# Routed tiles numbered by the token block of their first row, and the results of eight of sixteen token tiles gathered and added within the expert loop

## The reference, cut to what matters

```python
x = x + 0.5 * _L0_ffn_ref(_layernorm(x, axis=-1), ...)
x = x + _L0_attn_ref(_layernorm(x, axis=-1), ...)
x = x + 0.5 * _L0_ffn_ref(_layernorm(x, axis=-1), ...)
```

```python
scores = jax.nn.sigmoid(jnp.einsum('ed,btd->bte', gate_w, x)) + gate_b
weights, indices = jax.lax.top_k(scores, 4)
weights = weights / weights.sum(-1, keepdims=True)
shared_out = jax.nn.silu(x @ w1_shared) * (x @ w3_shared) @ w2_shared
h3 = jax.nn.silu(jnp.einsum('btd,edc->btec', x, w1_routed) * jnp.einsum('btd,edc->btec', x, w3_routed))
experts_out = jnp.einsum('btec,ecd->bted', h3, w2_routed)
return shared_out + jnp.einsum('bted,bte->btd', experts_out, router_probs)
```

## Time and profile before

| what | us |
|---|---|
| median of three runs | 695.49 |
| fastest and slowest run | 694.51, 701.63 |
| the profiled execution, span of the trace | 702.1 |
| VectorE, ScalarE, GpSimd, TensorE busy in it | 443.5, 372.6, 350.9, 509.0 |

### The profile page before, as it was taken

One profiled execution on the slowest core, in us unless ns is written; L12 is line 12 of the kernel. 1 busy time (PEld: TensorE's weight loads), 2 busy tenths in 40 slices (PEclk: granted clock), 3 DMA queues, 4 the chain that ended last, 5 costly groups with the idle time before them and its releaser, 6 DMA issues.

```text
span 702.1 us, 14339 instructions
## 1 busy us (share of the span) xinstructions
PE 509.0 (73%) x3204; PEld 462.6 (66%) x3205; DVE 443.5 (63%) x1453; ACT 372.6 (53%) x1132; POOL 350.9 (50%) x362
## 2 busy tenths in 40 slices
PE   4867699999999802538286924999999999632702
PEld 4845599999999801426264912999999999521501
DVE  5887477777777523448397587677777777221516
ACT  3777377777777701426175645677777777200000
POOL 2997544444444077464402233544444442475764
PEclk9987799999999955568599965899999999755555
DMA  9951254444445344232201440344444444433633
GB/s 304 392 201 51 83 152 134 134 131 128 131 133 129 102 130 126 82 113 74 77 0 35 144 167 15 99 134 135 128 130 132 134 125 113 132 115 92 177 98 105
DMA packets 61135, 88.11 MB, mean 126 GB/s; under 512 B 9499, under 2 KB 46363, under 8 KB 61107
## 3 DMA queue, kind: packets, MB, share of 16 engines
q0 software_dynamic: 13728, 37.50, 21.2%
q1 hardware_dynamic: 47379, 50.29, 20.8%
HBM read 57.22 MB, written 30.54 MB: 125 GB/s over the span
## 4 chain that ended last, share of the span: by engine, by line
PE 56%; DVE 13%; issue 9%; ACT 6%; DVEq 5%; another core or an unknown queue 4%; DMA 3%; POOL 3%; SPq 0%; ACTq 0%
PE bank L1164 26%; PE bank L1215 13%; PE bank L1186 5%; DVE xres L972 3%; PE bank L1379 3%; PE bank L1226 3%; PE bank L1225 3%; POOL mamba_room L488 2%; DVEq L972 2%; DVEq L971 1%; DVE lg L802 1%; DMA ys_scratch<-ring_f 1%; PE bank L1237 1%; DVE ring_f L948 1%
## 5 line engine op out<-in xcount | busy, mean ns | idle before, releaser
L478 POOL DMA_INDIRECT ring_f<-xn_scratch,tokidx x158 | 152.8, 967 | 170.3 <-PE bank L1186 150.0
L1164 PE MATMUL bank<-w_routed,ring_r 128*128 x948 | 194.6, 341 | 0.0
L488 POOL DMA_INDIRECT mamba_room<-ys_scratch,si x128 | 124.2, 971 | 97.3 <-issue 36.3
L1164 PEld LDWEIGHTS bank<-w_routed,ring_r 128*128 128x128 f32 x948 | 152.4, 192 | 1.0 <-issue 0.8
L1215 PE MATMUL bank<-w_routed,ring_r 128*128 x790 | 119.7, 282 | 0.7 <-DVE ring_r L832 0.6
L1215 PEld LDWEIGHTS bank<-w_routed,ring_r 128*128 128x128 f32 x790 | 110.1, 188 | 1.6 <-issue 1.6
L565 ACT ACTIVATE ring_r<-bank 128x256 fp32r<-128x256 f32 x158 | 60.8, 385 | 73.9 <-PE bank L1226 73.9
L972 DVE SCALAR_TENSOR_TENSOR xres<-mamba_room,wk,xres 128x256 f32<-128x256 f32 (+1 forms) x128 | 57.4, 481 | 52.5 <-issue 43.1
L830 DVE TENSOR_TENSOR ring_r<-bank,ring_r 128x128 fp32r<-128x128 f32 x158 | 46.1, 292 | 63.7 <-ACT ring_r L565 63.6
L822 DVE TENSOR_TENSOR ring_r<-bank,ring_r 128x256 fp32r<-128x256 f32 x158 | 67.1, 425 | 14.2 <-ACT ring_r L556 8.1
L1379 PE MATMUL bank<-mamba_room,stage 128*128 128x256 f32 (+1 forms) x144 | 42.5, 451 | 43.8 <-ACT mamba_room L754 30.0
(11 more groups left out here) (147 smaller groups left out, 755.6 us busy)
## 6 DMA issues: line engine op xcount, KB each, us to landing
ys_scratch<-ring_f SPq DMA_DIRECT2D x158, 128.0 KB
raw_routed<-in_w13r SPq DMA_DIRECT2D x6, 704.0 KB, 12.4
xn_scratch<-w_routed SPq DMA_DIRECT2D x32, 128.0 KB, 4.9
raw_routed<-in_w2r SPq DMA_DIRECT2D x6, 512.0 KB, 13.5
raw_routed<-in_w13r SPq DMA_DIRECT2D x8, 352.0 KB, 5.9
ring_f<-xn_scratch,tokidx POOLq DMA_INDIRECT x158
xres<-in_x_in SPq DMA_DIRECT2D x4, 512.0 KB, 6.2
raw_routed<-in_w2r SPq DMA_DIRECT2D x8, 256.0 KB, 7.3
```

The costliest lines, as they stand in the source:

```text
L478: pool.indirect_dma_start(xg[j % UN], None, xn_dram, bass.IndirectOffsetOnAxis(ap=tokidx[:, j:j + 1], axis=0)).then_inc(s_g[j % UN], 16)
L488: pool.indirect_dma_start(cg[t % 4][:, q, :], None, ys_dram, bass.IndirectOffsetOnAxis(ap=si[:, n:n + 1], axis=0)).then_inc(s_cg[t % 4][q] ...
L1164: last = pe.matmul(out, a, b, start=(q == 0), stop=(q == len(terms) - 1))
```

## The change: what it does

The slots are worked out otherwise. For each pair of an expert and a token block of 128 tokens the new route_slots finds how many tiles the expert begins in that block, and numbers the tiles in the order of these blocks, then of the experts. So the choices of the token blocks 0 to t lie in the first 4 (t + 1) + 15 tiles (tiles_before), and a token tile can be fetched once those are written. The number of tiles is 79 as before. The expert of a tile is found from a table of 256 places (teq has two halves, tile_experts two matmuls).

The 32 row sets of the token tiles 0 to 7 are fetched within the loop (fetch_early, into six buffers early_rows outside the room cg): set n after x gather 29 + 2 n, so one behind two x gathers, and seven of them (25 to 31) behind the last x gather. VectorE adds set n in its own step 32 + 2 n of the loop (row_added), the seven last ones behind it. Its loop is written out from step 29 on. The token tiles 8 to 15 are fetched as before, from the moment on which TensorE has done the last result (s_y), each with a wait for its own tiles. The output weights of the middle layer are loaded behind the loop, since two of the six buffers lie in their place. In f = 0 the pairs 0 to 3 have only the shared part left to add in the combine, in f = 1 likewise.

```diff
+        def tiles_before(t):
+
+            return min(NS, 4 * (t + 1) + NE - 1)
+
+        def written(f, b, n):
+
+            return 16 * (f * tiles_of(b, 2) + (n - b + 1) // 2)
+
+        def early_after(n):
+
+            return max(4 * (n // TOPK) + EARLY_FIRST, EARLY_FIRST + 2 * n)
+
+        def early_step(n):
+
+            return early_after(n) + EARLY_ADD
...
+            bodies = ((looped or count) - depth) // un
...
                 if f == 0:
+                    sp.wait_ge(s_ea, EARLY)
+                    sp.dma_start(stage[1][:, 0:512], wm_d[:, 1024:MW]).then_inc(s_wo, 16)
...
-                sp.wait_ge(s_cd, combined_to(1, t))
+                if t < EARLY_TILES:
+                    sp.wait_ge(s_sa, t // 2 + 1)
+                else:
+                    sp.wait_ge(s_cd, combined_to(1, t))
...
+            def fetch_early(f, n):
+
+                t, q = divmod(n, TOPK)
+                if q == 0:
+                    for b in range(2):
+                        pool.wait_ge(s_yw[b], written(f, b, tiles_before(t)))
+                if n >= ROWS:
+                    pool.wait_ge(s_ea, f * EARLY + n - ROWS + 1)
+                pool.indirect_dma_start(early_rows[n % ROWS], None, ys_dram[0:tiles_before(t) * P, :],
+                                        bass.IndirectOffsetOnAxis(ap=si[:, n:n + 1], axis=0)
+                                        ).then_inc(s_er[n % ROWS], 16)
...
             def combine(f, t):
 
-                if t >= 4:
+                for b in range(2):
+                    pool.wait_ge(s_yw[b], written(f, b, tiles_before(t)))
+                if t >= EARLY_TILES + 4:
                     pool.wait_ge(s_cd, combined_to(f, t - 4))
                 for q in range(TOPK):
                     n = t * TOPK + q
-                    pool.indirect_dma_start(cg[t % 4][:, q, :], None, ys_dram,
+                    pool.indirect_dma_start(cg[t % 4][:, q, :], None, ys_dram[0:tiles_before(t) * P, :],
                                             bass.IndirectOffsetOnAxis(ap=si[:, n:n + 1], axis=0)
                                             ).then_inc(s_cg[t % 4][q], 16)
 
...
                 for j in range(NS):
                     gather(f, j)
-                for b in range(2):
-                    pool.wait_ge(s_yw[b], 16 * tiles_of(b, 2) * (f + 1))
-                for t in range(NT):
+                    for n in range(EARLY):
+                        if early_after(n) == j:
+                            fetch_early(f, n)
+                for n in range(EARLY):
+                    if early_after(n) >= NS:
+                        fetch_early(f, n)
+                pool.wait_ge(s_y, (f + 1) * NS)
+                for t in range(EARLY_TILES, NT):
                     combine(f, t)
...
+                if pair == 0:
+                    act.wait_ge(s_ea, 2 * EARLY)
...
+                ones = cst[:, C_ONE:C_ONE + 1].broadcast_to((P, NT * NE))
+                up_to, before = whole_pad[:, :, 1:NT + 1], whole_pad[:, :, 0:NT]
+                link(dve.memset(segments, 1.0))
+                link(dve.memset(by_expert(segments)[:, :, 0], 0.0))
+                dve.memset(whole_pad[:, :, 0], 0.0)
+                dve.memset(current[:, 0:1], 0.0)
                 dve.wait_ge(s_cum, f + 1)
-                one = cst[:, C_ONE:C_ONE + 1]
-                link(dve.tensor_tensor_scan(gsum, one.broadcast_to((P, NT * NE)), p_tot, 0.0, ALU.mult, ALU.add))
-                link(dve.tensor_tensor(p_exc, gsum, p_tot, ALU.subtract))
-                gs3 = gsum.rearrange("p (e t) -> p e t", e=NE)
...
+
+                link(dve.tensor_tensor_scan(counted, segments, p_tot, 0.0, ALU.mult, ALU.add))
+                dve.tensor_tensor(p_first, counted, p_tot, ALU.subtract)
+                link(dve.tensor_scalar(p_up, counted, P / 2 - 0.5, ROUND, ALU.add, ALU.add))
+                link(dve.tensor_scalar(up_to, by_expert(p_up), ROUND, None, ALU.subtract))
+                link(dve.tensor_tensor(begun.rearrange("p (t e) -> p e t", e=NE), up_to, before, ALU.subtract))
+                dve.tensor_tensor(by_expert(rank), by_expert(p_first), before, ALU.subtract)
+                link(dve.tensor_tensor_scan(p_nth, ones, begun, 0.0, ALU.mult, ALU.add))
+                dve.tensor_tensor(by_expert(p_waiting), up_to, before, ALU.is_equal)
+                link(dve.tensor_tensor(by_block(p_past), by_block(p_pre), in_order(rank), ALU.add))
+                link(dve.scalar_tensor_tensor(by_expert(mine), begun.rearrange("p (t e) -> p e t", e=NE), 1.0 / P,
+                                              p_nth.rearrange("p (t e) -> p e t", e=NE), ALU.mult, ALU.mult))
+                dve.tensor_tensor(p_new, p_nth, begun, ALU.subtract)
+                link(dve.tensor_tensor_scan(current[:, 1:NE * NT + 1], p_waiting, mine, 0.0, ALU.mult, ALU.add))
+                dve.tensor_tensor(p_diag.rearrange("p (h s) -> p h s", h=2), mine.rearrange("p (h s) -> p h s", h=2),
+                                  ident.unsqueeze(1).broadcast_to((P, 2, P)), ALU.mult)
+                last_tile = in_order(current[:, 0:NE * NT])
+                dve.tensor_tensor(by_block(base_slot), by_block(p_past), last_tile, ALU.add)
+                link(dve.tensor_tensor(by_block(step_up), by_block(p_new), last_tile, ALU.subtract))
+                dve.tensor_reduce(place, p_diag.rearrange("p (h s) -> p h s", h=2), AX.X, ALU.add)
+                link(dve.scalar_tensor_tensor(taken, p_past, 0.0, step_up, ALU.is_ge, ALU.mult))
+                dve.tensor_scalar(place_tile, place, 1.0 / P, -1.0, ALU.mult, ALU.add)
                 sl = p_slot.rearrange("p (t e) -> p t e", e=NE)
-                link(dve.tensor_tensor(sl, p_pre.rearrange("p (t e) -> p t e", e=NE),
-                                       gexc.rearrange("p (e t) -> p t e", e=NE), ALU.add))
+                link(dve.tensor_tensor(p_slot, base_slot, taken, ALU.add))
+                dve.tensor_tensor(teq, i4[:, 0:NT_TE, 0].unsqueeze(1).broadcast_to((P, 2, NT_TE)),
+                                  place_tile.unsqueeze(2).broadcast_to((P, 2, NT_TE)), ALU.is_equal)
...
+            def add_early(f):
+                def stage(i, c):
+                    for n in range(EARLY):
+                        if early_step(n) == c + LAG_T + 1:
+                            row_added(f, n)
+                return stage
+
+            def row_added(f, n):
+
+                t, r = n // TOPK, n % ROWS
+                dve.wait_ge(s_er[r], 16 * rows_fetched(f, n))
+                if n % TOPK:
+                    dve.wait_ge(s_ea, f * EARLY + n)
+                dve.scalar_tensor_tensor(xres[:, t, :], early_rows[r], wk[:, n:n + 1], xres[:, t, :],
+                                         ALU.mult, ALU.add).then_inc(s_ea, 1)
...
                 else:
-                    for b in range(2):
-                        dve.wait_ge(s_cg[2 * c + b][TOPK - 1], 16 * (i + 1))
+                    late = 2 * pair >= EARLY_TILES
+                    for b in range(2 if late else 0):
+                        dve.wait_ge(s_cg[(2 * pair + b) % 4][TOPK - 1], 16 * fetches(0, 2 * pair + b))
                     for b in range(2):
                         add_fetched(2 * pair + b)
+                    for q in range(TOPK if late else 0):
+                        for b in range(2):
+                            add(0, 2 * pair + b, q, done + 2 * q + b + 1)
+
+            def combine_last(pair):
...
+                dve.wait_ge(s_sy, pair + 1)
+                dve.scalar_tensor_tensor(xp, p_yS[pair % 2][:, :], 0.5, xp, ALU.mult, ALU.add).then_inc(s_sa, 1)
+                if 2 * pair < EARLY_TILES:
+                    return
+                dve.wait_ge(s_sa, pair + 1)
+                for t in range(2 * pair, 2 * pair + 2):
                     for q in range(TOPK):
+                        add(1, t, q, combined_before(1, t) + q if q else None)
...
-                pipeline(dve, NS, [(LAG_H + 1, dve_product(base)), (LAG_T + 1, dve_ht(f)), (LAG_X, dve_x(base))])
+                pipeline(dve, NS, [(LAG_H + 1, dve_product(base)), (LAG_T + 1, add_early(f)), (LAG_T + 1, dve_ht(f)),
+                                   (LAG_X, dve_x(base))], looped=EARLY_FIRST)
+                for n in range(EARLY):
+                    if early_step(n) >= NS + LAG_T + 1:
+                        row_added(f, n)
+                dve.wait_ge(s_ea, (f + 1) * EARLY)
                 if f == 1:
-                    with dve.Fori(0, NT // 4) as i:
-                        for c in range(2):
-                            combine_last(i, c)
+                    for pair in range(NT // 2):
+                        combine_last(pair)
...
-                    pe.wait_ge(s_wm, 32)
+                    pe.wait_ge(s_wm, 16)
...
+                        if c == 0:
+                            pe.wait_ge(s_wo, 16)
```

120 lines of the change are left out of this document (57 added, 63 removed).

## The result

On the chip of the first comparison the change gives 686.4 us (median of 14 runs, 682.3 to 691.6) against 696.3 (14 runs, 690.6 to 702.2): ratio 0.985, 95% interval 0.982 to 0.988. I had said 636, with a range of 606 to 676. The profiled execution has a span of 685.7 us against 702.1. GpSimd's rows cut both executions into the same six stretches.

The account below looks back on a forecast made before the run. TensorE was taken to bound the loops, and waits, partly on late signals, the two combining stages. 702.1 - 36 (last stage) - 37 (middle layer) + 2 (loops) + 11 (routing) = 642, less 6.6 gives 636 us; range 606 to 676.

Parts of the forecast that it names:

- The loops: Both expert loops: 32 added gathers and adds each nearly fit the step, plus 1 us each (0 to 3).
- Rival A: Expert loops: GpSimd's 94% duty brings late signals between engines into them, making the kernel slower; chance 0.17.
- mild form: Expert loops: late signals cost 0.2 us a step, 50 steps twice, giving 656 us.
- dear form: Expert loops: signals stop after each 10 us until GpSimd has run dry, plus 126 us, 762 us.
- Rival B: Expert loops: add and gather lock each other out, 4.68 us per two steps, plus 35 us, 671 us; chance 0.03.
- Last stage: Stage behind the second loop: 32 combine gathers instead of 64, started earlier, some late signals remaining: minus 36 us.
- 42 if only the buffers bind: Last stage: gain in us if GpSimd waits only for free buffers and no signal is late.
- Middle layer: Between the loops: earlier first combine, fewer gathers and adds, 14 us of late signals: minus 37 us (51 to 27).
- Routing: Slot computation in both layers: longer VectorE chain and collisions with GpSimd, plus 5 and plus 6 us.
- The offset: Whole kernel: median of the runs lies 6.6 us under the profiled execution's span, carried over to the forecast.
- C: Both combining stages: late signals stay as they were, plus 9 and plus 25 us, 670 us; chance 0.10.
- D: Both combining stages: late signals vanish, minus 51 and minus 42 us with the same routing, 616 us; chance 0.06.

Follow-up runs that it names:

- chip 8: Another chip on which the unaltered change and the kernel before were both run and profiled: 625.3 us against 666.3, ratio 0.940.
- r1: Changed kernel with the early adds on one column of 256, gathers and waits kept: 684.0 us where the kernel before took 699.4.
- r2: Changed kernel with early rows fetched by plain SyncE DMAs of a fixed block instead of GpSimd gathers, adds full size: 646.1 us, kernel before 699.4.
- s3: Changed kernel with four early token tiles instead of eight, one row set per four x gathers: 712.6 us, kernel before 699.1.
- e2: Changed kernel without early gathers, full-size adds reading a resident token tile: 624.1 us, kernel before 665.6.
- e1: Changed kernel with the early adds on one column of 256, gathers and waits kept: 627.9 us, ratio 0.943, kernel before 665.6.
- e4: Changed kernel with early rows fetched by plain SyncE DMAs of a fixed block instead of GpSimd gathers: 630.6 us, kernel before 665.6.
- r3: Changed kernel with the last stage's shared-expert pairs reordered (4, 0, 5, 1, 6, 2, 3, 7): 696.1 us, ratio 0.994, kernel before 699.4.
- s2: Changed kernel with GpSimd pausing behind the loops until each token tile's last row set has landed: 690.7 us, kernel before 699.1.

## Why the prediction was wrong

- **The loops, "plus 1 us each", is the step that failed.** It measured 17.0 and 19.2 us, 34 of the 50 us between 636 and 686. I had costed GpSimd's time (it fits: on three chips the loop stays at 1.99 us a step), VectorE's gap and the lead of the x gathers, all rightly, as chip 8 shows. The term for late signals in the loop was nothing. Against them I had put that nothing was late there so far and that GpSimd must pause as soon as TensorE stalls, and behind both stood my reading that signals come late only when a row has lasted some 10 us, taken from long rows alone. r1, r2 and s3 show that on such a chip a row of three, 3.5 us, is enough: 0.70 us a pair, 1.1 us where the rows are fewer.
- **Rival A was the mechanism, at 0.17.** Its mild form had 0.2 us a step and 656 us; measured is 0.35 us a step. Its reasoning against itself, that GpSimd must pause when TensorE stalls, is why it stayed mild: GpSimd's idle time before a gather is 1.2 us in every pair, and the signal is through 0.86 us after the row. The dear form did not come.
- **Rival B had the price and not the mechanism.** Its 4.68 us a pair met the 4.70 measured. r1 takes the add away and the pair stays, r2 keeps it and the pair goes. Had I stopped at the agreement of two numbers, the explanation would have been false. What I held against it was weak, too: of the last eight adds, 0.58 us apiece (4.66 / 8), only those of the first 1.3 us lie beside a gather. An add took 0.47 to 0.48 us beside a gather's issue on chip 8, and as much in e2, which has no early gather. The rule I quoted from the Trainium skill (SBUF — State Buffer, section Who interferes with whom) doesn't contradict this: it has such an add contend only with a GpSimd instruction that reads SBUF. The routing agrees with its first half: two steps with both operands in SBUF took 1.72 and 1.73 us while GpSimd worked on the weights' low parts.
- **Last stage, -36 against -33.3.** Right in its mechanism, and without late signals right in size: "42 if only the buffers bind" leaves 73.5 us, and e1 and e4 take 74.6. On the first chip it is late by 6.7 us at its start (last x gather to first combine gather 21.5 us, not 14.8). The waits of the last early sets for writes and buffers are on chip 8 too, where this takes 15.3 us; the rest is late signals at the loop's end, for which I had put nothing. The 3 us that I had added for late signals in the last 16 gathers did not come. ScalarE goes on when the row of six gathers (to 608.17) is over:

```profile
608.20 0.38 ACT L639 ACTIVATE ring_r<-bank 128x256 fp32r<-128x256 f32 x1 [4.47 <-remote]
```

- **Middle layer, -37 against -32.6.** My 331 without late signals is 101.8 us after the last x gather, and chip 8 took 101.7. On the first chip the stretch is 18.8 us longer than there, instead of the 14 I took for late signals (TensorE's clock is lower, too, 0.78 against 0.87): again at the loop's end (22.5 us from the last x gather to the first combine gather, 15.2 on chip 8), and one wait of 6.9 us later instead of two of 11. GpSimd stood still for 22.7 us in between, as forecast.
- **Routing, +11 against +13.2.** Chains of 13.5 and 12.7 us, within my 9 to 14.
- **The offset.** I took 6.6 us off, the profiled execution's distance to the median. The changed kernel's median lies 0.7 us above its profiled span: 7.3 us of the 50 are this.
- **C and D** fit neither kind of chip. On the first, late signals shrank but did not stay (C) or vanish (D). C's price was mis-added: 17 us twice less the 5.6 in my forecast is plus 28 and not 25, so 673. On chip 8 there were none before the change either, so there was less to gain in the stages that wait; the loops' forecast was right there, and the kernel gained 41 us by the medians.

Why some chips hold signals back and others do not, no run shows. Nor is it settled why a row of four with 2.6 us behind it harms nothing in the last stage, while three with 1.1 to 1.3 us behind them harm the loop: the length of the pause and the density of signals both differ.

## What to carry to other kernels

An effect that a profile shows as idle time for which nothing on the page accounts should be priced wherever the change brings its cause, even at a fraction of the dose, and before a stage is called bound by its engine. Two numbers that agree do not name a mechanism: take each suspect away alone, on a chip that shows the effect. Look at the clock of a stretch before you put its length down to the change: the last stage of one execution on chip 8 is 9 us short, at a clock of 0.82 instead of 0.67. And compare kernels on more than one chip: here the same change is worth 1.5% on one and 6% on another, and an order of pairs that gains 1% more on the second kind loses 1% on the first.

## What the runs showed of the hardware

- Chips differ by more than the change is worth. The kernel before took 696.3, 699.4 and 699.1 us on three chips and 665.6, 666.3 and 665.5 on three others, each in one session. Its two profiles, one from each kind, have equal durations of the loops' instructions (a gather 0.97 and 0.96 us, L1164's matmul 0.34 in both).
- On the slow kind, while GpSimd issues indirect gathers in a row, TensorE's signals reach ScalarE and GpSimd late: 0.86 to 0.97 us after the end of a row of three. In a row of 32 ScalarE idled up to 18.4 us and VectorE up to 14.2 us for them (r3). DMAs of as many bytes from SyncE's queue in the same places of the loop do not do this (r2).
- Leaving half of the early gathers out made it worse, not better, for each that was left: 1.1 us against 0.70 (s3).
- TensorE's clock sets the last stage: a pair of token tiles of the shared expert takes 5.32 us where the granted clock is 0.50 (e1, s2) and 3.1 us where it is 1.00 (the changed kernel on chip 8).
